# A decoder layer on one core: residual rows of the first two norms through TensorE, their sums on ScalarE, and an earlier start for GpSimd's product

## The reference

```
x = layernorm(x + mamba(x))          # norm 1
x = layernorm(x + xattn(x, ctx))     # norm 2
x = layernorm(x + ffn(x))            # norm 3

mamba(x):  hidden, gate = split(x @ W_in)             # 1024 channels each
           hs = silu(causal conv over 4 rows of hidden + conv_bias)
           dt, B, C = split(hs @ W_x)                 # 128, 16, 16
           dts = softplus(dt @ W_dt + b_dt)
           state[t] = exp(dts * A) * state[t-1] + dts * B * hs   # 1024 channels x 16 states
           y = (sum over states of state * C + hs * D) * silu(gate)
           return y @ W_out
xattn(x, ctx): att = softmax((ctx @ Wq.T + bq) @ (ctx @ Wk.T + bk).T); return x . att   # out[l,m] = sum_n x[l,n] att[m,n]
ffn(x):    int8 quantized product of x and weight, rescaled, plus bias
```

## Time and profile before

| | |
|---|---|
| timed runs | 1085.72, 1086.15 and 4713.28 us; median 1086.15 us |
| the profiled execution, its own time | 1085.01 us |
| its span (first to last instruction) | 1083.1 us |
| granted clock of PE, mean share of full | 0.899 |
| busy: DVE / PE / ACT / POOL | 94% / 79% / 73% / 62% of the span |

### The profile page before, as it was taken

How to read it: one execution, slowest core, us unless ns; L and a number is a source line. 1 busy time by engine, 2 the same in 40 slices (tenths; PEclk the granted TensorE clock), 3 DMA queues, 4 the chain that set the end, 5 groups by cost and what they waited for, 6 DMA issues and landing times.

```text
span 1083.1 us, 10459 instructions
## 1 busy us (share of the span) xinstructions
PE 850.6 (79%) x2958; PEld 334.8 (31%) x2968; DVE 1017.7 (94%) x861; ACT 790.7 (73%) x1171; POOL 667.3 (62%) x260
## 2 busy tenths in 40 slices
PE   8945788786799899687599899887699475755985
PEld 3321233231233344232134344332133132222432
DVE  3699999999999998999999998999999999999746
ACT  4486687776766898997766898998676695876524
POOL 1056666666676766776667756786766766776343
PEclk9987798898899899999899999988799778877998
DMA  6354445453743444343743453343833532243001
GB/s 195 83 129 109 107 115 127 106 135 103 204 110 75 128 117 125 82 123 87 232 115 97 127 126 98 78 117 102 243 88 87 156 93 72 68 138 85 11 0 40
DMA packets 58474, 120.08 MB, mean 111 GB/s; under 512 B 12208, under 2 KB 18480, under 8 KB 58416
## 3 DMA queue, kind: packets, MB, share of 16 engines
q1 hardware_dynamic: 57696, 119.34, 41.9%
q10 hardware_dynamic: 720, 0.08, 0.1%
HBM read 48.07 MB, written 4.19 MB: 48 GB/s over the span
## 4 chain that ended last, share of the span: by engine, by line
DVE 32%; issue 29%; PE 19%; ACT 9%; DMA 4%; POOL 4%; SPq 2%; DVEq 0%; POOLq 0%; ACTq 0%
DVE st L768 20%; PE dense L876 12%; DVE dBu L760 7%; ACT dA L551 4%; PE dense L913 3%; POOL st L445 3%; DMA rep<-steps 2%; PE dense L944 2%; ACT L551 2%; DMA out<-x 2%; SPq L357 1%; DVE dense L859 1%; DVE xsc L824 1%; DVE x L706 1%; DVE steps L746 1%
## 5 line engine op out<-in xcount | busy, mean ns | idle before, releaser
L445 POOL TENSOR_TENSOR st<-st,Cb 128x2048 f32<-128x2048 f32 x127 | 575.1, 4528 | 368.1 <-DVE dBu L760 263.3
L768 DVE TENSOR_TENSOR_SCAN st<-dA,dBu 128x1024 f32<-128x1024 f32 x256 | 570.2, 2268 | 0.4 <-ACT dA L551 0.4
L551 ACT ACTIVATE dA<-rep,Aneg 128x511 f32<-128x511 f32 x512 | 329.2, 712 | 54.4 <-DVE st L768 49.6
L760 DVE TENSOR_TENSOR dBu<-rep,Bb 128x1024 f32<-128x1024 f32 x256 | 324.1, 1310 | 1.9 <-DMA rep<-steps 1.9
L876 PE MATMUL dense<-xTs,Win 128*128 128x512 f32 x504 | 236.4, 615 | 13.5 <-ACT wide L556 6.6
L913 PE MATMUL dense<-st,sel 128*32 128x512 f32 x1024 | 138.7, 689 | 64.5 <-POOL st L445 63.0
L876 PEld LDWEIGHTS dense<-xTs,Win 128*128 128x128 f32 x504 | 98.7, 199 | 142.8 <-issue 141.8
L876 PE MATMUL dense<-wide,hs 128*128 128x512 f32 x256 | 115.8, 605 | 6.7 <-ACT xTs L671 4.5
L944 PE MATMUL dense<-pj,Win 128*128 128x512 f32 (+1 forms) x192 | 94.8, 640 | 18.9 <-issue 18.5
L551 ACT ACT_TABLE_LOAD x75 | 96.2, 1283 | 17.4 <-DVE st L768 16.3
L913 PEld LDWEIGHTS dense<-st,sel 128*32 128x32 f32 x1024 | 33.4, 124 | 167.4 <-issue 91.2
(11 more groups left out here) (110 smaller groups left out, 733.6 us busy)
## 6 DMA issues: line engine op xcount, KB each, us to landing
rep<-steps SPq DMA_DIRECT2D x512, 128.0 KB, 2.4
Win<-w_in SPq DMA_DIRECT2D x64, 256.0 KB, 2.9
wide<-w_out SPq DMA_DIRECT2D x4, 2048.0 KB, 10.1
Win<-w_conv SPq DMA_DIRECT2D x24, 256.0 KB, 2.9
xTs<-xT SPq DMA_DIRECT2D x3, 1024.0 KB, 5.7
x<-x SPq DMA_DIRECT2D x3, 1024.0 KB, 6.0
out<-x SPq DMA_DIRECT2D x12, 256.0 KB, 2.0
wide<-w_x SPq DMA_DIRECT2D x4, 640.0 KB, 4.9
```

The costliest lines, as they stand in the source:

```text
L445: nc.gpsimd.tensor_tensor(s, s, Cb[:], ALU.mult).then_inc(s_p, NH)
L551: nc.scalar.activation(dA[:, u % 2, j, 1:T], rep[:, u % REPS, 0, 1:T], ACT.Exp, scale=Aneg[:, u % UNITS, j:j + 1]).then_inc(s_dA, 1)
L760: V.tensor_tensor(dBu[:, j, :], rep[:, u % REPS, 1:2, :].to_broadcast([P, JH, T]), Bb[:, j, :], ALU.mult).then_inc(s_mul, 1)
L768: V.tensor_tensor_scan(st[:, u % RING, j, :].rearrange("p j t -> p (j t)"), dA[:, u % 2, j, :].rearrange("p j t -> p (j t)"), dBu[:, j, :] ...
```

## The change

Six edits. DVE no longer touches the first two norms of the batches 0 to 2:

1. `wo`, batches 0 to 2: PE adds the residual rows with one more matmul, identity times rows, ahead of the eight of the product; the wait for the loaded rows moves from DVE to PE.
2. `at`, all batches: in place of four transposes PE does four matmuls against the identity and a fifth, identity times identity, onto the diagonal block, so that `av` contains the residual.
3. `wo` and `av`, batches 0 to 2: ACT evicts the product into the rows, with the sum of each row in `accum_out`; DVE has no instruction for them.
4. `av`, last batch: DVE evicts with `copy_rows`, which no longer reads the rows.
5. POOL's wait ahead of L445: in units without `step_inputs` it waits for the first of the two products L760 of the next unit, in units with them for both; the wait for `step_inputs` goes.
6. The tables `REST`, `HID_AT` and `CONV_AT` put several items into other steps.

```diff
-REST = {"wo": [2, 3, 7, 8], "q": [5], "k": [1], "en": [7, 9, 10, 11], "at": [10, 12, 14, 14],
-        "xt": [13, 13, 15, 17], "av": [15, 17, 19, 19], "qt": [17, 20, 22, 23], "ff": [19, 21, 23, 27]}
+REST = {"wo": [3, 3, 6, 8], "q": [2], "k": [1], "en": [5, 9, 10, 11], "at": [10, 12, 14, 14],
+        "xt": [13, 13, 14, 15], "av": [15, 17, 19, 19], "qt": [18, 20, 22, 23], "ff": [19, 22, 23, 25]}
-HID_AT = [6, 9, 10, 13, 15, 17, 21, 23]
-CONV_AT = [9, 10, 13, 14, 17, 18, 22, 24]
+HID_AT = [5, 9, 11, 13, 14, 17, 19, 22]
+CONV_AT = [9, 10, 13, 14, 17, 18, 21, 24]
...
                     pool.wait_ge(s_scan, NH * (u + 1))
-                    pool.wait_ge(s_mul, NH * (u + 2))
-                    pool.wait_ge(s_du, step_inputs_before(u + 2))
+                    if step_inputs_at(u + 1):
+                        pool.wait_ge(s_mul, NH * (u + 2))
+                    else:
+                        pool.wait_ge(s_mul, NH * (u + 2) - 1)
...
+                    elif kind in ("wo", "av") and kb < LAST:
+                        ps, free = full(key)
+                        n = norm[key]
+                        nc.scalar.activation(rows_of[kb][:, i, :], ps, ACT.Identity,
+                                             accum_out=rowsum[:, n % 4:n % 4 + 1]).then_inc(free, 1)
...
+            def copy_rows(key, x_i, ps, free):
+                n = norm[key]
+                if n >= 4:
+                    normalized(dve, norm_keys[n - 4])
+                V.tensor_scalar(x_i, ps, 1.0, 0.0, ALU.mult, ALU.add,
+                                accum_out=rowsum[:, n % 4:n % 4 + 1]).then_inc(free, 1)
...
+                    elif kind in ("wo", "av") and kb < LAST:
+                        if kind == "av":
+                            norms.setdefault(s + QUANT_LAG, []).append(key)
...
+                        elif kind == "av":
+                            copy_rows(key, x_i, ps, free)
...
+            def turned_plus_one(key, src, i):
+                ps, done = bank_of(key)
+                for k in range(KH):
+                    mm = nc.tensor.matmul(ps[:, k * P:(k + 1) * P], src[:, k * P:(k + 1) * P], ident[:],
+                                          start=True, stop=k != i)
+                    if k == i:
+                        mm = nc.tensor.matmul(ps[:, k * P:(k + 1) * P], ident[:], ident[:], start=False, stop=True)
+                mm.then_inc(done, 1)
...
-                        product(key, [(hs[:, kb % 2, e, cols], Wout[:, e, :]) for e in range(first, end)])
+                        rows = []
+                        if kb < LAST:
+                            if i == 0:
+                                pe.wait_ge(s_xr, 16 * (kb + 1))
+                            rows = [(ident[:], rows_of[kb][:, i, :])]
+                        product(key, rows + [(hs[:, kb % 2, e, cols], Wout[:, e, :]) for e in range(first, end)])
...
-                        turned(key, att_of[kb][:, i % 2, :])
+                        turned_plus_one(key, att_of[kb][:, i % 2, :], i)
```

## The result

The changed kernel took 1061.2 us in the median of four runs (1060.8 to 1061.8), the kernel before 1085.9 beside it (one of its runs, at 4713 us, is a disturbed one). The ratio is 0.9774 with a 95% interval of 0.9755 to 0.9793, so 2.1 to 2.5% faster. Predicted were 1058 us, in a range of 1046 to 1074.

The account below looks back on a forecast made before the run. DVE, busy 94% of the span, was taken to bound the kernel, with ACT and PE nearly as full in two stretches. Saved 40.6 us, given back 13, left 27.6: 1058 us predicted, range 1046 to 1074.

Parts of the forecast that it names:

- The port step: POOL's product, released by the first L760, ends before the next L760 pair; the 0.34 us stall behind scans vanishes.
- The term of 18.5: In L760: about 55 pairs stalled 0.34 us each by POOL's product, all saved by the earlier release, 18.5 us.
- The 1 us that L474 was to give: Three L474 delay L760 by 1.08 us each, 3.2 in all; 1 us of it counted as saved.
- The adds: 24 L706 leave DVE, saving 14.6 us and 6.5 of waits for PE; ACT gets 24 evictions, 0.87 us each.
- The note on `copy_rows`: Last batch's eviction reads one operand less, on PSUM, where nothing says it is faster: 4 x 0 to 0.1 us.
- The wait at 1017: Last batch: DVE's 6.08 us wait for the state sum, from PE's queue of wp and at, stays; 1 us more there.
- The idle term: In two full stretches DVE alone would gain 9.5 us each, but 6 each is given back, 12 in all.
- the stretch: 354 to 485 us (steps 9 to 24, batch 1), likewise 602 to 732 in batch 2: DVE, ACT, PE full at once.
- Rival B: ACT and PE take all the gain of the full stretches, and step 3 its 3 us: 1068.5 us, chance 0.12.
- step 3 with its 18.9 us of PE: Two wo and a gate share this step, leaving PE no slack: 0 to 1 us lost in each of three batches.
- The part on the tables: Edit 6: the moved items spread the load, except in step 3; one more ACT table load of 1.28 us in three batches.

Follow-up runs that it names:

- both reliefs: changed kernel with exponential for silu in the convolution's eviction of batches 1 to 3, and two of four attention matmuls left out in batches 0 to 2: 1048.05 us.
- first_half_always: changed kernel with POOL's product released by the first of the two products in every unit, those with step_inputs too: 1117.4 us, ratio 1.028.
- av_halved: changed kernel without two of the four matmuls of each attention product in batches 0 to 2: 1061.25 us, ratio 0.9776.

## Why the prediction was right, and where a term was off

**The port step held in its mechanism.** L760's mean was predicted at 1225 to 1235 ns and came out at 1236, the pair behind scans at 2.36 and came out at 2.34, POOL's recorded product at 5.3 us (median 5.327) and 4.7 with `step_inputs` (4.8). The term of 18.5 for about 55 short stalls was 18.9 for 57, and none is left. The 1 us that L474 was to give did not come: three long stalls of 3.2 us together became five of 3.9. With the median of an undisturbed product at 1221 in place of 1225 ns, L760 lost 18.9 us in all; the edit alone gave 19.7 us of time. What is left, (1236 - 1221) x 256 = 3.8 us, is for the larger part this, once in each of the batches 1 to 3 (timeline of DVE):

```profile
450.34 3.29 DVE L776 TENSOR_TENSOR dBu<-rep,Bb 128x1024 f32<-128x1024 f32 x2
```

There POOL has the norms of three rows and a bias add ahead of its product and is through 1.1 us into the pair, which takes 3.29. In batches 1 and 2 there is a second one, of 0.58 us, beside a bias add.

**The adds.** 24 L706 went, and with them their waits for PE. DVE's busy time fell by 32.9 us where the terms of busy time made 34.1. ACT's eviction was priced by L664 at 0.68; it took 0.59, since it has no bias to read or for another reason that no run separates. The note on `copy_rows` was right: 692 ns (L722) against 691 for the add. The wait at 1017 stayed, 6.12 us against 6.08. Rows of both, in DVE's timeline and groups:

```profile
993.40 0.69 DVE L750 TENSOR_TENSOR hs<-dense,ta 128x512 f32<-128x512 f32 x1 [6.12 <-PE dense L944]
...
L722 DVE TENSOR_SCALAR_CACHE_REDUCE hs<-dense 128x512 f32<-128x512 f32 x4 | 2.8, 692 | 6.3 <-PE dense L897 6.3
...
L722 DVE DVE_READ_ACCUMULATOR hs<-dense 128x1 f32 x4 | 0.3, 83 | 0.0
```

**The idle term was too small.** The step that failed is "the stretch becomes ACT's: at least 125, at most the 131 of now. I take 127.5". ACT's need was over- and not underestimated (121.9 us and not 125.0), PE's right (118.1 for 118.5), DVE's nearly (122.4 for 121.5), and yet the stretch took 132.2, beyond the upper bound. A stretch is not as long as its fullest engine: DVE stood idle for 9.6 us in it while neither PE nor ACT was full, and only both reliefs together took most of that away. Part of the miss is edit 6: with the old tables the stretch is 129.3, inside the bounds and still 1.8 above the 127.5. Rival B's "ACT and PE take all the gain of the full stretches" is what happened there.

**What made up for it, by luck.** In the forecast the two stretches gain 3.5 us each, 7.0 together, and all the rest 20.6. Measured are a loss of 3.5 and a gain of 27.6: 10.5 us too few inside, 7.0 too many outside. Each error is larger than the 3 us by which the total is off. Outside, DVE's busy time fell by 25.1 us, where 34.1 less 5.6 for each stretch is 22.9, and its idle time by 2.5 more, all of it in the last batch, where the forecast had 1 us given back. Rival B's other parts did not come: step 3 with its 18.9 us of PE cost nothing (the four units that contain it in batch 2 took 27.7 us against 29.3). In the ledger of the loop, from the first L760 to the end of the last scan: 34.1 us of busy time were to go and 6.5 of idle time to come; 33.0 went and 9.2 came (17.1 to 26.3). 27.6 predicted, 23.7 in the loop, 24.1 in the span.

**The part on the tables** ("the moved items spread the load") is not borne out: the old ones do at least as well. The new ones do remove one wait of PE, that in step 22, but they put others in its place.

## What to carry to other kernels

Compare an instruction's mean with its median before you move work off the busiest engine: here 22 of its "busy" us were waiting for GpSimd's product, and a wait released one instruction earlier, so that GpSimd stands in line behind the last instruction that collides with it and ahead of none, gave some four fifths of the gain. Where engines with fixed lists feed each other, neither sums of busy time nor the relief of one engine tell how long a stretch takes; look for the hand-over that stands at the head of one list and deep in the other. Of the versions tried, the changed kernel with the old tables is the fastest that computes the same, by a margin that is near what can be measured.

## What the runs showed of the hardware beyond expectation

- GpSimd's product that comes up during an instruction of VectorE with two SBUF operands is recorded with its standing included: 5.33 us in place of 4.53. It ends 4.36 us after that instruction, 0.17 less than its undisturbed duration.
- When GpSimd's product has stood for some 0.9 us behind an instruction of VectorE, and VectorE's next one with two SBUF operands follows at once, the outcome varies: of 25 such `step_inputs` in `first_half_always`, 14 waited for the whole product (up to 5.06 us) and 11 not at all (0.68 to 0.69 us, the product then 5.95).
- A relief can coincide with a slower clock: in `av_halved` the granted clock of PE fell to half from 676.2 to 679.6, 0.6 us after PE had ended a standstill of 3.5 us, and the product there took 5.37 us in place of 3.60. DVE then waited 5.0 us for the next state sum, against 2.4 in the other full stretch of the same run, where the clock stayed up.
